# The start of an eight-layer transformer kernel: who fills a constant, where the first norm stands, and how the second batch's queries reach their rows

## The reference

```python
x = x + _L0_xcond_ref(_layernorm(x), ctx, ctx, tau, delta, Wq, bq, Wk, bk, Wv, bv, Wo, bo)
x = x + _L0_ffn_ref(_layernorm(x), ...)     # 16 experts, top 4
... # L1: the same attention, 8 experts, top 1; L2: local attention, a small transformer layer; L3: attention, gated experts
# the attention, with 16 heads of 8:
scores = einsum('bhqd,bhkd->bhqk', q, k) * tau + delta
p_attn = softmax(scores / sqrt(8))
out = einsum('bhqk,bhkd->bhqd', p_attn, v) @ Wo.T + bo
```

## Time and profile before

| | |
|---|---|
| median of 3 runs | 1052.99 us (1052.76 to 1057.67) |
| the profiled execution | 1051.74 us |
| its span, first to last instruction | 1049.9 us |
| mean granted TensorE clock | 0.828 |
| first score product of unit (0,0) | at 46.27 us |
| first score product of unit (0,1) | at 76.63 us |

### The profile page before, as it was taken

One profiled execution on the slowest core, in us unless ns is written; L12 is line 12 of the kernel. 1 busy time (PEld: TensorE's weight loads), 2 busy tenths in 40 slices (PEclk: granted clock), 3 DMA queues, 4 the chain that ended last, 5 costly groups with the idle time before them and its releaser, 6 DMA issues.

```text
span 1049.9 us, 13386 instructions
## 1 busy us (share of the span) xinstructions
PE 751.1 (72%) x3940; PEld 466.1 (44%) x3940; DVE 621.5 (59%) x1995; ACT 344.6 (33%) x584; POOL 261.2 (25%) x305
## 2 busy tenths in 40 slices
PE   2578772848849657577585745876887678689998
PEld 1123331848838412223373634474654323245554
DVE  6657756326224435666442536789786767666764
ACT  2455420524415234233221112212232365432231
POOL 4050366440242371710323032212111100000000
PEclk9589865869959867767796876898998899789999
DMA  5135021433523340206112010010210111000000
GB/s 162 46 103 209 18 80 62 124 93 109 151 83 87 106 109 11 70 27 215 50 42 83 21 38 1 1 68 4 70 34 13 45 58 33 1 1 11 11 11 10
DMA packets 70784, 64.87 MB, mean 62 GB/s; under 512 B 9076, under 2 KB 62637, under 8 KB 70202
## 3 DMA queue, kind: packets, MB, share of 16 engines
q1 hardware_dynamic: 53178, 47.36, 15.4%
q0 software_dynamic: 5120, 10.50, 3.4%
q10 hardware_dynamic: 12416, 6.16, 2.0%
HBM read 34.94 MB, written 22.54 MB: 55 GB/s over the span
## 4 chain that ended last, share of the span: by engine, by line
PE 46%; DVE 24%; issue 16%; ACT 4%; POOL 3%; SPq 3%; DMA 1%; another core or an unknown queue 1%; DVEq 0%; ACTq 0%; POOLq 0%
PE psum_all L884 5%; PE psum_all L900 5%; DVE s_nmx L1325 3%; PE psum_all L796 3%; PE psum_all L778 3%; PE psum_all L780 3%; PE psum_all L691 3%; PE psum_all L669 3%; PE psum_all L671 2%; PE psum_all L650 2%; DVE s_x_normed L1226 2%; PE psum_all L766 2%; PE psum_all L606 2%; DVE s_h L1463 1%; PE psum_all L744 1%
## 5 line engine op out<-in xcount | busy, mean ns | idle before, releaser
L2493 POOL TENSOR_SCALAR s_vare<-s_mv 128x4 f32<-128x4 f32 x40 | 11.8, 295 | 456.3 <-DVE s_mv L1218 456.2
L1325 DVE TENSOR_REDUCE s_nmx<-psum_all 128x4 f32<-128x308 f32 x192 | 83.3, 473 | 58.8 <-PE psum_all L650 36.1
L2078 ACT ACTIVATE s_hT<-psum_all 77x1024 f32<-77x1024 f32 x96 | 95.8, 1017 | 65.2 <-PE psum_all L671 44.1
L650 PE MATMUL psum_all<-s_ks,s_t 128*128 128x308 bf16 x192 | 61.1, 365 | 52.2 <-DVE s_nmx L1325 27.5
L669 PE MATMUL psum_all<-s_t,s_ks 128*77 128x512 bf16 x192 | 85.2, 444 | 11.4 <-ACT s_hT L2078 8.5
L671 PE MATMUL psum_all<-s_t,s_ks 128*77 128x512 bf16 x192 | 83.7, 436 | 0.0
L1583 DVE COPY s_t<-s_arena 128x256 f32 x94 | 21.6, 292 | 99.4 <-remote 47.4
L2413 POOL DMA_INDIRECT s_w<-routed_y,s_cT x64 | 61.9, 967 | 72.7 <-issue 72.7
L691 PE MATMUL psum_all<-s_hT,s_v 77*32 77x512 f32 x384 | 61.1, 711 | 25.2 <-ACT s_hT L2078 24.1
L900 PE MATMUL psum_all<-s_arena,s_hT 128*128 x376 | 62.8, 303 | 22.0 <-issue 21.6
L2399 POOL DMA_INDIRECT routed_x<-s_x_normed,s_cT x64 | 63.2, 987 | 47.5 <-DVE s_cT L1522 28.7
(11 more groups left out here) (315 smaller groups left out, 1578.6 us busy)
## 6 DMA issues: line engine op xcount, KB each, us to landing
s_t<-q_parts SPq DMA_DIRECT2D x60, 128.0 KB, 2.9
routed_y<-s_hT ACTq DMA_DIRECT2D x22, 256.0 KB
s_ks<-s_att SPq DMA_DIRECT2D x72, 77.0 KB, 2.1
s_arena<-in_w SPq DMA_DIRECT2D x2, 2048.0 KB, 11.9
q_parts<-s_qparts SPq DMA_DIRECT2D x10, 384.0 KB
s_h<-routed_x SPq DMA_DIRECT2D x48, 64.0 KB
s_x_normed<-routed_x SPq DMA_DIRECT2D x46, 64.0 KB
routed_x<-s_w SPq DMA_DIRECT2D x34, 64.0 KB
```

What stands on the lines that cost most here:

```text
L650: pe.matmul(o, T1[:, u % QS, g, 128 * i:128 * i + 128], KS1[:, HPG * g:HPG * g + HPG, SK * b:SK * b + SK], start=True, stop=True))
L1325: read(job, dve.tensor_reduce(nmx[:, u % 2, i, HPG * g:HPG * g + HPG], PS[:, k, 0:HPG * SK].rearrange("p (h s) -> p h s", h=HPG), AX.X, AL ...
L2078: read(("S", L, b, p), nc.scalar.activation(Eexp[:, (PAIRS * u + p) % ES, :, :], PS[0:SK, k:k + 2, :], ACT.Exp))
```

## The change

DVE's `keys(0)` ends with the split, and the 12 blocks move into a stage `blocks` behind the statistics of batch 0. The same stage computes `tscale`, and waits for the rows that hold `tau`. PE makes the values ahead of `front`; DVE adds their bias behind `norm`. ACT fills the ones of `T1` with three activations of scale 0 and bias 1. Batch 1's projection leaves the prologue: PE issues it in unit (0,0) behind the first two score pairs, ACT scales it at step 0, DVE splits it at step 0, and SP places it with `place_q`. A list `FIRST_PLACES` replaces `plan` for unit (0,0). ACT's copy of `pick7` moves into step 3 of that unit.

```diff
 }
+FIRST_PLACES = [((0, 0, 0), "Q", 0, 1), ((0, 0.5, 0), "stats", 0, 3), ((1, 0, 1), "front", 0, 2), ((3, 3, 0), "M0", 0, 1),
+                ((4, 4, 0), "M1", 0, 1), ((2, 2.5, 2), "Q", 0, 2), ((5, 5, 0), "M2", 0, 1), ((6, 6, 0), "M3", 0, 1),
+                ((7, 6.5, 7), "MT", 0, 1), ((0, 7, 0), "norm", 0, 3)]
...
             which = ("pe", "dve", "act").index(engine)
+            if u == (0, 0):
+                return sorted([(at[which], *x) for at, *x in FIRST_PLACES], key=lambda x: x[0])
             if u in LATE_PLACES:
...
-        BEFORE = ([(stage, 0, 0) for stage in ("keys", "stats", "norm", "front", "values", "Q", "M0", "M1")]
+        BEFORE = ([(stage, 0, 0) for stage in ("keys", "stats", "blocks", "norm", "values", "front", "Q", "split", "M0", "M1")]
                   + [("stats", 0, 1)] + [(stage, 0, 0) for stage in ("M2", "M3", "MT")]
-                  + [(stage, 0, 1) for stage in ("norm", "front", "Q")] + [("stats", 0, 2), ("norm", 0, 2)])
+                  + [(stage, 0, 1) for stage in ("norm", "front")] + [("stats", 0, 2), ("norm", 0, 2)])
...
-        QD = [nc.dram_tensor(f"q_parts{u}", (P, 3, SQ), BF16, kind="Internal").ap() for u in range(2, len(attn_units))]
+        QD = [nc.dram_tensor(f"q_parts{u}", (P, 3, SQ), BF16, kind="Internal").ap() for u in range(1, len(attn_units))]
...
         def t1_placed(eng, u):
-            eng.wait_ge(s_t1[u], 16 * (12 if u < 2 else 3))
+            eng.wait_ge(s_t1[u], 16 * (12 if u < 1 else 3))
...
         def t2_placed(eng, u):
-            eng.wait_ge(s_t2[u], 16 * (12 if u < 2 else 3))
+            eng.wait_ge(s_t2[u], 16 * (12 if u < 1 else 3))
...
-            if u < 2:
+            if u < 1:
                 t1_placed(eng, u)
...
             else:
-                eng.wait_ge(s_qd, 16 * (u - 1))
+                eng.wait_ge(s_qd, 16 * u)
...
                     pe.wait_ge(s_drow, 16 * 3)
-                    pe.wait_ge(s_pool0, 4)
+                    pe.wait_ge(s_pick, 2)
                 for g in groups:
...
                 scores(1)
+                if u == 0:
+                    project_q(0, 1)
                 for p in range(PAIRS):
...
                 pe.wait_ge(s_w["m7"], 16 * 3)
-                pe.wait_ge(s_pick, 2)
+                pe.wait_ge(s_pick, 3)
...
             def stage_of(stage, L, b):
-                if stage in ("stats", "norm", "slots", "rows", "combine0", "combine1") or (stage == "values" and LAYERS[L] == ROUTED):
+                if stage in ("stats", "norm", "blocks", "split", "slots", "rows", "combine0", "combine1") or (stage == "values" and LAYERS[L] == ROUTED):
                     pass
...
                     (mha_front if LAYERS[L] == MHA else front)(L, b)
+                elif stage == "Q" and (L, b) != (0, 1):
+                    project_q(L, b)
                 elif stage == "Q":
-                    project_q(L, b)
+                    pass
                 elif stage == "MT":
...
                     dve.wait_ge(s_ks[a - 1], 16 * 12)
+                    key_blocks()
+            def key_blocks():
                 mask = const("head_mask")
...
                     values(0)
+                elif stage == "blocks":
+                    key_blocks()
+                    dve.wait_ge(s_rows, 16 * 4)
                     link(dve.tensor_scalar(tscale[:, 0, :], row("tau"), ATT_SCALE, None, ALU.mult))
...
                     ins.then_inc(s_tau, 1)
+                elif stage == "split" or (stage == "Q" and (L, b) != (0, 0)):
+                    split_q(L, b)
                 elif stage == "Q":
-                    split_q(L, b)
+                    pass
                 elif stage == "MT":
...
                 stage_of(*x)
-                if x[0] == "Q":
-                    u = x[2]
-                    dve.wait_ge(s_q3, u + 1)
+                if x[0] == "split":
+                    dve.wait_ge(s_q3, 1)
                     for part in (1, 2):
                         for g in range(2 - part, NG):
-                            dve.tensor_copy(T1[32 * part:32 * part + 32, u, g, :],
-                                            qparts[32 * g:32 * g + 32, part, :]).then_inc(s_t1[u], 16)
+                            dve.tensor_copy(T1[32 * part:32 * part + 32, 0, g, :],
+                                            qparts[32 * g:32 * g + 32, part, :]).then_inc(s_t1[0], 16)
             for n, (L, b) in enumerate(units):
...
             nc.scalar.copy(KS2[96:128, :, :], const("pick_head")[96:128, :].unsqueeze(2).to_broadcast([32, NH, CK])).then_inc(s_pick, 1)
+            some = const("pick_head")[96:128, 0:1].unsqueeze(2).to_broadcast([32, NG, SQ])
+            for u in range(QS):
+                ins = nc.scalar.activation(T1[96:128, u, :, :], some, ACT.Identity, scale=0.0, bias=1.0)
+            ins.then_inc(s_pick, 1)
             for x in BEFORE:
...
-                    u = x[2]
                     act.wait_ge(*slots.is_read(x))
                     for g in range(NG):
-                        nc.scalar.copy(T1[0:32, u, g, :], qparts[32 * g:32 * g + 32, 0, :]).then_inc(s_t1[u], 16)
-                    act.wait_ge(s_q3, u + 1)
-                    nc.scalar.copy(T1[32:64, u, 0, :], qparts[0:32, 1, :]).then_inc(s_t1[u], 16)
-            act.wait_ge(s_rows, 16 * 4)
-            nc.scalar.copy(pick7[:, :], H5[0:64, 0:GLU_PAIRS, :].rearrange("p a b -> p (a b)")).then_inc(s_pick, 1)
+                        nc.scalar.copy(T1[0:32, 0, g, :], qparts[32 * g:32 * g + 32, 0, :]).then_inc(s_t1[0], 16)
+                    act.wait_ge(s_q3, 1)
+                    nc.scalar.copy(T1[32:64, 0, 0, :], qparts[0:32, 1, :]).then_inc(s_t1[0], 16)
             for n, (L, b) in enumerate(units):
...
                             stage_of(*x)
+                    if step == 3 and (L, b) == (0, 0):
+                        act.wait_ge(s_rows, 16 * 4)
+                        nc.scalar.copy(pick7[:, :], H5[0:64, 0:GLU_PAIRS, :].rearrange("p a b -> p (a b)")).then_inc(s_pick, 1)
                     if step == 5 and LAYERS[L] == ATTN:
...
             ins.then_inc(s_pool0, 1)
-            pool.memset(T1[96:128, :, :, :], 1.0).then_inc(s_pool0, 1)
-            pool.wait_ge(s_pool0, 4)
+            pool.wait_ge(s_pool0, 3)
             pool.memset(r_zeros, 0.0).then_inc(s_rz, 1)
...
                 pool.wait_ge(s_rtab, 16 * 3)
-                pool.wait_ge(s_pick, 2)
+                pool.wait_ge(s_pick, 3)
                 pool.memset(r_ones, 1.0)
...
                 sp.wait_ge(s_q3, u + 1)
-                sp.dma_start(QD[u - 2], qparts[:, :, :]).then_inc(s_qd, 16)
-                sp.wait_ge(s_qd, 16 * (u - 1))
-                by_row = QD[u - 2].rearrange("(g r) j c -> j r g c", g=NG)
+                sp.dma_start(QD[u - 1], qparts[:, :, :]).then_inc(s_qd, 16)
+                sp.wait_ge(s_qd, 16 * u)
+                by_row = QD[u - 1].rearrange("(g r) j c -> j r g c", g=NG)
                 for j in range(3):
...
-            for u in range(2):
-                sp.wait_ge(s_q3, u + 1)
-                place_queries(u, T2, (0, 1, 0), s_t2[u])
+            sp.wait_ge(s_q3, 1)
+            place_queries(0, T2, (0, 1, 0), s_t2[0])
+            place_q(1)
             sp.dma_start(r_upper_in, A["upper"]).then_inc(s_rtab, 16)
...
                 routed_clear(0, range(x, x + TPB))
-            sp.wait_ge(s_pick, 2)
+            sp.wait_ge(s_pick, 3)
             for n in range(3):
...
```

## The result

| | before | after |
|---|---|---|
| median of 20 runs each, same chip | 1056.36 us | 1044.69 us |
| ratio, 95% interval | | 0.990 (0.9875 to 0.992) |
| span of the profiled execution | 1049.9 us | 1040.5 us |
| mean granted TensorE clock | 0.828 | 0.823 |
| first score product of unit (0,0) | 46.27 | 37.42 |

The kernel is 1.0% faster (0.8 to 1.25%). The forecast was 0.66% (1052.99 to 1046.0) with a range of 1040.5 to 1054; 1044.7 lies inside. Both marks came early, the first by 8.85 us and the second by 11.14. Here and further down a median is over all runs of a kernel, while a ratio leaves out the executions that took over 1.5% more than the fastest of their kernel.

A forecast was written before the change was run, and what follows sets the result against it. DVE, standing behind POOL's fill, was taken to bound the prologue. The first score gains 8.1 us, one goes to the unit, leaving 7: 1051.74 becomes 1044.7, plus 1.25 for the median, 1046.0; range 1040.5 to 1054.

The forecast's parts named there:

- The fill and the port: Prologue: without POOL's fill, DVE's delta scale takes some 0.35 us and `keys` starts at 6.9 instead of 10.62, 3.7 us earlier.
- The blocks beside POOL: Prologue: DVE's 12 blocks, overlapping POOL's variance and power, were taken to lose 1.0 us, within bounds of 0 and 1.4.
- Rows 7: Profile rows cited: four norm operations that take 1.11 us alone took 3.90 beside three POOL operations of 1.26 us.
- The first score: Start of unit (0,0): first score product at 38.2 instead of 46.27, 8.1 us earlier, with `T2`'s landing the last wait.
- Unit (0,0): First attention unit: M0 of batch 1 at 57.5, second unit's first score at 69.7 instead of 76.63, 7 us earlier.
- the windows of 109 to 116: Profile windows before: PE with 62% busy over 109 to 112 stood at 1.00, then fell to a mean of 0.57.
- the first half of the new unit ... like the second of these: Unit (0,0) before M0: three gaps of 1.5 to 2.5 us, busy some 60%, likened to the 109 to 112 window.
- the upper level all through: Rival: TensorE's clock stays up in unit (0,0), second unit at 66.1, 10.5 us less, 1042.5; chance 0.15.
- From M0 on the term: Second half of unit (0,0): 10.2 us instead of 8.7, with 3 us at the lower clock level, then 2.0 for MT.
- The placing: Batch 1's queries in unit (0,0): split ends at 46.6, store and loads take 6.6, so `T1` lands at 53.2, before M0.
- the 3 us given for the later changes of level: Rest of the run: some twenty changes of clock level, moved against the work, can give or take 3 us.
- POOL's tables: Unit (0,0): 9.0 us of tables start at some 57, batch 3's power is ready at 67.5, hidden from DVE.

The follow-up runs named there:

- e1: The changed kernel with the ones of T1 filled by POOL again in one fill; 1056.74 us, ratio 0.997 to the kernel before.
- e5: The kernel before with POOL's fill of the ones cut into three, one per buffer of T1; one run, 985.65 us.
- e7: The changed kernel with POOL's wait for the landed rows moved behind the first power; 968.82 us, ratio 0.983 to the kernel before.
- e8: e7 with statistics, norm and turn of batch 1 ahead of M0, and T2 of batch 0 placed by a store and three loads; 964.37 us, ratio 0.979.
- e11: The changed kernel with batch 1's maxima and their turn one step earlier in unit (0,0); 976.32 us, ratio 0.997 to the kernel before.
- e6: The changed kernel with batch 1's queries placed by the old copies and 12 DMAs, still projected inside unit (0,0); 977.59 us, ratio 0.999.
- e3: The kernel before with ScalarE's fill and the new order, batch 1's queries still projected in the prologue and placed by copies; 1056.85 us, ratio 0.996.
- e2: The changed kernel with batch 0's old prologue order: blocks ahead of statistics, turn ahead of values, query scale behind the values' bias; 1052.22 us, ratio 0.9905.
- e10: e8 with GpSimd's addition of the bias row to batch 1 put behind the variance and power of batch 2; 968.99 us, ratio 0.989.
- e12: e10 with the edit of e11, batch 1's maxima one step earlier; 978.62 us, ratio 0.996 to the kernel before.
- e9: The changed kernel run again unaltered, on the third chip; 967.12 us, ratio 0.987 to the kernel before.

## Why the prediction was right, and where it was off

**The fill and the port, right.** The scale under 0.6 us (0.31); `keys` at 6.9 (7.13); the statistics done by 10.4 (10.7). e1 and e5 show the cause.

**The blocks beside POOL, wrong side.** I took 1.0 us for DVE, from the row in which DVE stood behind POOL; DVE lost nothing, and POOL 0.2 to 0.4 (after 0.22, e1 0.34, e7 0.24). That was the side for which I had cited the page "SBUF — State Buffer" of the Trainium skill, "Who interferes with whom": whichever engine comes second blocks. e5, e7 and e8 show both sides of it here: a scale or cast of DVE against one long POOL operation loses up to all of that (5.0, 1.58, 1.37 us), POOL's small operations against twelve short blocks lose 0.05 to 0.4 each (the variance 0.36 in e11). Length alone does not tell the cases apart: POOL's power is no short operation (1.04), and DVE's three scales for `tscale` beside it in after took 0.51, as against 0.49 before, where nothing lay beside them. Rows 7 had a size, but for wide additions. Two errors offset each other, which is luck: the rows landed at 12.8, not 12.0, and the norm waited for POOL, not for DVE, so it was at 14.51 (predicted 14.8), ACT's scaling at 19.59 (19.8).

**The first score, right to 0.8 us.** 37.42 against 38.2: the first maximum was placed by 37.1 (37.4), `T2` landed at some 37.3 instead of 38.2, since the key copies began at 13.26 (14.1), and PE's own turn of batch 1 ended at the same time. That `T2`'s landing was the last wait holds in e7; in after it is not shown.

**Unit (0,0), the mis-sized term.** I gave 19.3 us from the first score to M0 of batch 1 (38.2 to 57.5), between the upper level (17.2) and the lower (22.0), and it took 16.0 (37.42 to 53.43). The clock rose at 39.8, within the first scores, and stayed up through three gaps of 1.6 to 2.5 us with PE busy for 58%. I had read the windows of 109 to 116 as a sign that such a stretch brings it down. So the step "the first half of the new unit ... like the second of these" failed, and the rival "the upper level all through", 0.15 by me, was the nearer case for the mark. Of the 3.3 us too many, 1.2 lie ahead of the end of the second exponential (7.5 predicted, 6.3 measured, with the projection at 1.02 where I took 1.6), and 2.1 behind it: 11.8 predicted, midway between the levels, and 9.7 measured, which is the upper level's own price. By the page of the Trainium skill that I cited against myself ("TensorE: Matmul & The Clock Gate", "HAM oscillation — how this bites in real kernels"), only long idleness brings the level down; 39.8 to 53.5 agrees, and so do e11, whose fall lies in a wait of 4.70 us, and e6, whose fall follows one of 5.08. The fall at 53.5 in after came 1.1 us behind a gap of 2.53 us, and the one behind 109 to 112 behind gaps of 0.6 us at most. From M0 on the term was right: 12.2 predicted, 12.06 measured, 3.4 us of it at the lower level where 3 were assumed. That this phase has 3 us of it was a guess between two cases, so the close hit is in part luck; in e7, with M0 at 54.47, the first half took 17.3 and the second 10.9.

**The placing.** `T1` landed by about 51 and was no wait, as forecast (53.2 before 57.5). By e6, 6.3 of the 11.1 us go when the old copies come back, and by e3 6.6 when the deferral goes too. So the deferral alone is worth 0.4 with the old copies; whether the new placing needs it was not tested. The fill and the order bring 3.4 and 3.1 at the first score; at the second unit 3.3 and 3.1 (e1, e2), 1.3 of the order's 3.1 being the rows' late landing in e2. Together with the placing that is 13, against 11.1 for all. The parts don't add up; the changes of level, which fall elsewhere in each kernel, are the likely reason, and are not separated.

**The sum.** 1051.74 less 11.1 is 1040.6; the profiled execution took 1042.3. The 7 us of the forecast would have made 1044.7. By medians 11.7 us were gained, not 7. That 1044.69 lies so near to the 1046.0 forecast is in part luck: the forecast started from a median of three runs of the kernel before, 1052.99, and over twenty it is 1056.36. What is gained at 65 us is thus found again at the end, within the 3 us given for the later changes of level; that single executions wander by more (the lead is 13.8 us at layer 2) was not foreseen. There, within layer 1, two waits of DVE that the profile puts down to another core or an unknown queue take 47.4 us before and 36.0 after. POOL's tables were hidden (55.2 to 63.0, power of batch 3 done at 64.4), though the norm behind it shows a wait of 0.36.

**Which mark tells the time.** On the second and third chip the ratios fall in two groups: 0.979 to 0.989 where the second unit starts at 65 to 66 us (e7 to e10), and 0.996 to 0.999 where it starts at 71.8 to 75.0 (e6, e11, e12). The first score does not sort them: e12 has the earliest (35.28) and 0.996. On the first chip the order is less clean: e1 and e2 share the mark (68.8 and 68.6) and have 0.997 and 0.9905, with intervals that overlap, so a single ratio can't tell 3 us.

**Open.** Why layer 1 took 50 to 60 us less on the second and third chip: in the profiles of before and after engines wait there for something that the profile puts down to another core or an unknown queue, and in e9's there is no such wait. And what brings the level down at 53.5. That e7 or e8 beats the changed kernel is not shown: 0.983 and 0.979, from four runs each, come from another chip than e9's 0.987, the intervals overlap, and e10, the mended e8, ties with e9 on the same chip.

## What to carry to other kernels

Read a DVE operation that is far too long for its size against the end of the GpSimd operation beside it, and give long fills to ScalarE. When a stage is moved into a unit, take its copies off the engine that sets that unit's pace: with them the move was worth 0.4 us, without them 6.6 (e3, e6). Before an in-order TensorE is made to wait earlier, count what stands behind the wait at half the clock too, and look at what the same edit puts ahead of the last exponential: of e11's 9.5 us, 5.2 came by the first and 4.3 by the second.
